# Causal attention without mask matmuls: VectorE adds the mask while it takes the maxima, GpSimd zeroes the weights of later keys

## The chip, the cores and the metric

The kernel runs on one core of one Trainium2 chip. The metric is the device time of one execution in microseconds (us), and lower is better. The core has five engines with a queue each: TensorE (PE, matmuls; PEld is its loading of weights), VectorE (DVE), ScalarE (ACT), GpSimd (POOL) and SyncE (SP, which issues most of the DMAs). Engines wait for each other only through semaphores. Matmul results go to PSUM, of which there are eight banks of 128 x 512 f32; everything else that is computed on lies in SBUF.

## What is computed

The reference is a model of four layers, each an attention-like mixer and a feed-forward part, on 4 sequences of 512 tokens with 128 channels. The change concerns the attention of the second layer (16 heads of 8 channels), which is causal: a query sees its own key and the earlier ones. It is softmax attention, with scale = 8 ** -0.5:

```
x = _layernorm(x + _L1_attn_ref(x, L1_attn_q_heads, L1_attn_k_heads, L1_attn_v_heads, L1_attn_output_proj), axis=-1)

scores[q, k] = (Q[q] . K[k]) * scale,   for k <= q alone
weights      = softmax over k of scores
output[q]    = sum over k of weights[q, k] * V[k],   then the output projection
```

The second block sums the attention up; the first line is the reference's own. The third and the fourth layer have attentions of the same size without causality (one with a bias by distance, one with an additional key).

## The kernel before

The stream of attention work is laid out in **units**: a unit is one sequence and four heads, so there are 16 units in each of the three attentions. A unit has eight **jobs** (128 jobs in all), each for one tile of 128 queries or keys and two of the four heads. Work is written out in **slots** t from -14 to 133. In slot t the engines' queues get:

- *maxima of job t + 14* (`maxima`): TensorE multiplies 128 queries (tile `qt`) by the keys up to the end of that tile, for two heads, into two PSUM banks (line 849). VectorE reduces both banks at once to the negated maximum of each row (line 1663, tile `negm`). The maxima are taken from coarser bf16 parts and only keep the exponentials in range.
- *turned maxima*, once a unit: GpSimd splits the maxima of a unit in a high and a low bf16 part (lines 2508 and 2510, `max_rows`), TensorE transposes them (line 859), VectorE copies the result to SBUF (line 1677), and a DMA from GpSimd's queue (line 2535, `row_of_maxima`) puts them as two rows into the query operands, so that the score matmul subtracts the maximum itself.
- *scores of job t* (`scores`): TensorE multiplies 128 keys (tile `kt`) by the queries from that tile on, one matmul a head (line 876). Keys lie on the partitions, queries along the bank. ScalarE takes the exponential of each head (line 1299) into the SBUF tile `PB`.
- *values*, in odd slots (`values`): TensorE multiplies the weights of the key tile of the jobs t - 3 and t - 2 by V with a column of ones, four heads side by side (line 892), accumulating over the four key tiles in bank 7. After the fourth, ScalarE copies the bank out (line 1312), TensorE turns it (line 900), and VectorE divides by the sum (lines 1693 and 1695, `output`).

Causality is done on TensorE. Where a product touches the diagonal tile, a further matmul of the identity (`b_ident`) by a 128 x 128 mask of 0 and -1e30 adds the mask to the bank: `b_causal_qk` after the maxima's matmuls (line 852, two a job), and `b_causal_kq` after each score matmul (line 879, two a job). The masks are loaded and cast to bf16 by GpSimd at the start of the kernel (`half_masks`, line 2274). `b_causal_kq` and `b_alibi_kq` have both the line 879; the latter belongs to the third layer's attention.

The maxima, the turned maxima and the outputs share a **ring** of two entries of two banks each (banks 0 to 3): the use number n needs the entry of use n - 2 freed by VectorE (semaphore `ring_free`; TensorE counts with `ring_filled`). The scores go round three banks (4 to 6), freed by ScalarE's exponentials (`exped`). `PB` is double buffered by key tile: ScalarE waits for the values two key tiles back (`valued`).

Each engine's queue is in order, and what stands in it is decided by the slots alone. In the last third of the stage other work is woven in by tables of slots (`inside1`): projection and normalisation of the three sequences that are done, the routing of their tokens to experts on VectorE, and on GpSimd scatters of token rows to DRAM by indirect DMA (lines 2342 and 2355), one a slot in the slots 93 to 100 and 105 to 112, with a copy at slot 104 that waits for the first eight (line 2348), and again from slot 125. The normalisation's inverse root is GpSimd's too (lines 2230 and 2232).

## Time and profile before

| | |
|---|---|
| median of 3 timed runs | 1177.18 us (1175.18 to 1180.2) |
| span of the profiled execution | 1195.9 us |
| difference of the two | 18.7 us |
| busy, share of the span | PE 85%, DVE 65%, ACT 55%, POOL 30% |
| chain of work that ended last, by engine | PE 67%, DVE 14%, ACT 8% |
| masks' matmuls in that chain (lines 879 and 852) | 3% and 2% |
| mean granted TensorE clock | 0.916 |

For the profiled execution the profile gives no time but its span, from the first to the last instruction. It is longer than the timed runs. All durations that are read from the trace belong to the profiled execution. In the rows, times are in us from the start of the span, unless marked ns; a group of instructions is named by its line in the kernel, its engine and operation, and what it writes and reads.

### The profile page before, as it was taken

To read this page: it belongs to the slowest core of one execution; us is meant where nothing else is said; L and a number is where in the kernel's file an instruction comes from. 1 tells how busy PE (TensorE), PEld (TensorE's weight loads), DVE (VectorE), ACT (ScalarE), POOL (GpSimd) and SP (SyncE) were. 2 spreads that over 40 slices of the span, in tenths; PEclk is the share of its full clock that TensorE was granted. 3 is DMA by queue.
4 is the path that set the end of the run, shared out by engine and by line. 5 is a ranking of instruction groups with operands and counts; after the bars stand their busy time and mean duration, and the time that the engine had idled before them with its cause. 6 is when DMAs were issued, how large, how long until landed. Compare 5 with 4: busy or idle time off the path is not lost.

```text
span 1195.9 us, 18814 instructions
## 1 busy us (share of the span) xinstructions
PE 1013.1 (85%) x6456; PEld 502.9 (42%) x6517; DVE 779.4 (65%) x1614; ACT 662.2 (55%) x1282; POOL 363.6 (30%) x587
## 2 busy tenths in 40 slices
PE   5599789999979899456999999798999998876993
PEld 2267534544436566332333333485323232233551
DVE  5966486768733300388888885429888889646565
ACT  4664536655544345152777777582477776753341
POOL 7535411101532244320000002210112223556554
PEclk9799779999988899865999999898799999999897
DMA  5910224334611120233333220003333423212232
GB/s 142 181 46 1 94 86 144 126 113 129 168 38 36 55 67 18 65 95 126 100 117 125 65 79 5 1 1 126 112 119 119 134 89 96 63 33 62 56 87 80
DMA packets 98374, 101.70 MB, mean 85 GB/s; under 512 B 13354, under 2 KB 80571, under 8 KB 98199
## 3 DMA queue, kind: packets, MB, share of 16 engines
q1 hardware_dynamic: 86169, 89.28, 25.3%
q0 software_dynamic: 6432, 8.18, 2.4%
q10 hardware_dynamic: 5680, 3.04, 0.9%
q8 instruction: 53, 0.87, 0.3%
q14 instruction: 40, 0.33, 0.1%
HBM read 66.60 MB, written 38.09 MB: 88 GB/s over the span
## 4 chain that ended last, share of the span: by engine, by line
PE 67%; DVE 14%; ACT 8%; issue 5%; DMA 3%; another core or an unknown queue 1%; POOL 1%; SPq 0%; ACTq 0%; DVEq 0%; POOLq 0%
PE PS L892 13%; PE PS L876 12%; PE PS L849 8%; PE PS L698 6%; PE PS L703 6%; DVE negm L1663 5%; PE PS L1170 4%; PE PS L1053 3%; PE PS L879 3%; PE PS L1047 2%; PE PS L852 2%; ACT arena L1299 2%; PE PS L900 2%; PE PS L1186 2%; ACT arena L1226 1%
## 5 line engine op out<-in xcount | busy, mean ns | idle before, releaser
L1299 ACT ACTIVATE arena<-PS 128x512 f32<-128x512 f32 (+3 forms) x768 | 363.0, 549 | 190.6 <-PE PS L879 121.8
L1663 DVE TENSOR_REDUCE negm<-PS 128x2 f32<-128x1024 f32 (+3 forms) x384 | 405.2, 1088 | 94.3 <-PE PS L849 46.1
L876 PE MATMUL PS<-arena 128*128 128x512 bf16 (+3 forms) x707 | 221.1, 363 | 12.1 <-ACT arena L1299 8.0
L892 PE MATMUL PS<-arena,VPAD 128*32 128x512 f32 (+3 forms) x1536 | 187.7, 559 | 0.1
L849 PE MATMUL PS<-arena 32*128 32x512 bf16 (+3 forms) x768 | 144.3, 376 | 33.1 <-DVE negm L1663 27.4
L849 PEld LDWEIGHTS PS<-arena 32*128 32x128 bf16 x768 | 36.3, 91 | 216.7 <-DVE negm L1663 112.9
L876 PEld LDWEIGHTS PS<-arena 128*128 128x128 bf16 x768 | 69.9, 98 | 123.5 <-issue 57.3
L2508 POOL CAST nmp<-negm 128x16 bf16<-128x16 f32 x48 | 9.3, 195 | 363.9 <-DVE negm L1663 244.1
L698 PE MATMUL PS<-arena,W 128*128 128x512 f32 x144 | 83.2, 711 | 11.5 <-ACT arena L1217 9.0
L703 PEld LDWEIGHTS PS<-W,arena 128*128 128x128 f32 x640 | 81.0, 206 | 13.8 <-issue 6.3
L703 PE MATMUL PS<-W,arena 128*128 128x128 f32 x640 | 82.8, 291 | 3.3 <-DVE arena L1607 3.0
L1170 PE MATMUL PS<-VPAD,arena 128*128 x92 | 53.3, 663 | 11.4 <-DVE arena L2174 5.5
L2535 POOL DMA_DIRECT2D arena<-mT x48 | 30.7, 639 | 101.1 <-DVE mT L1677 78.9
L1937 DVE TENSOR_TENSOR arena<-PS,arena 128x512 f32<-128x512 f32 x8 | 5.5, 692 | 84.2 <-PE PS L1053 84.2
L879 PE MATMUL PS<-b_alibi_kq,b_ident 128*128 128x128 bf16 x256 | 56.9, 222 | 4.0 <-issue 2.2
L2473 POOL DMA_INDIRECT rows_y<-arena,name x46 | 46.6, 1013 | 37.4 <-DVE arena L2187 17.9
L1407 ACT ACTIVATE arena<-PS,eb 128x320 f32<-128x320 f32 x64 | 33.8, 527 | 39.9 <-PE PS L1047 38.0
L2391 POOL DMA_INDIRECT rows_y<-arena,back x40 | 39.2, 981 | 54.6 <-DVE arena L1940 40.0
L879 PE MATMUL PS<-b_causal_kq,b_ident 128*128 128x128 bf16 x256 | 52.5, 224 | 2.8 <-issue 2.1
L1217 ACT COPY arena<-PS 128x512 f32<-128x512 f32 x39 | 22.7, 587 | 48.8 <-PE PS L694 45.3
L1047 PE MATMUL PS<-arena,VPAD 128*128 128x320 f32 x128 | 44.2, 472 | 3.4 <-ACT arena L1402 1.7
L698 PEld LDWEIGHTS PS<-arena,W 128*128 128x128 f32 x144 | 29.3, 225 | 41.9 <-issue 26.0
(334 smaller groups left out, 1541.3 us busy)
## 6 DMA issues: line engine op xcount, KB each, us to landing
arena<-score_q SPq DMA_DIRECT2D x48, 288.0 KB
arena<-score_k SPq DMA_DIRECT2D x48, 288.0 KB
arena<-max_parts SPq DMA_DIRECT2D x48, 256.0 KB
max_parts<-arena SPq DMA_DIRECT2D x36, 256.0 KB, 2.9
score_k<-arena SPq DMA_DIRECT2D x36, 128.0 KB
score_q<-arena SPq DMA_DIRECT2D x12, 384.0 KB
arena<-rows_y SPq DMA_DIRECT2D x16, 256.0 KB, 4.3
arena<-slots SPq DMA_DIRECT2D x46, 65.0 KB
```

The lines of the kernel that those rows point to most:

```text
L698: pe.matmul(bank(b), w, x, start=True, stop=True).then_inc(*T.did(c, name))
L703: mm = pe.matmul(PS[:, b, j * D:(j + 1) * D], lhs(f, j), rhs(f), start=(f == 0), stop=(f == nf - 1))
L849: mm = pe.matmul(PS[:, b + i, 0:nk], MQ[s][rows, qt * P:(qt + 1) * P], MK[s][rows, 0:nk], start=True, stop=True)
L876: mm = pe.matmul(PS[:, b, q0:S], OK[s][:, r, kt * P:(kt + 1) * P], OQ[s][:, r, q0:S], start=True, stop=True)
L879: mm = pe.matmul(PS[:, b, kt * P:(kt + 1) * P], bf["ident"][:], bf[o["kq"]][:], start=False, stop=True, skip_group_check=True)
L892: mm = pe.matmul(PS[32 * r:32 * r + 32, 7, q0:S], VP[:, u, kt, r, :], PB[:, kt % 2, r, q0:S], start=(kt == 0), stop=True, skip_group_check ...
L1047: pe.matmul(PS[:, (L.A, L.B)[h], 0:HALF], W1E[:, e, n * P:(n + 1) * P], L.exT[:, h * HALF:(h + 1) * HALF], start=True, stop=True).then_inc ...
L1170: pe.matmul(bank(2 * (t % 3) + 1), xT3[t % 4], WE3[:, bass.ds(experts[t] * 768, 512)], start=True, stop=True).then_inc(multiplied3, 1)
L1299: act.activation(PB[:, kt % 2, r, q0:S], PS[:, 4 + use % 3, q0:S], ACT.Exp, scale=slope(u % G, r) if o["slope"] else 1.0).then_inc(exped, 1)
L1663: vec.tensor_reduce(negm[:, u % 2, 2 * rp:2 * rp + 2, qt], PS[:, 2 * (use % 2):2 * (use % 2) + 2, 0:nk], AX.X, ALU.max, negate=True).then_ ...
L2391: pool.indirect_dma_start(rows_y, bass.IndirectOffsetOnAxis(ap=lanes[k].back[:, r, j:j + 1], axis=0), lanes[k].ey[:, j, :], None, bounds_c ...
L2473: pool.indirect_dma_start(rows_y, bass.IndirectOffsetOnAxis(ap=name3[:, i:i + 1], axis=0), y3[i], None, bounds_check=2 * B * S - 1, oob_is ...
```

## The change

The mask matmuls of the causal attention go, both kinds, and with them the masks `b_causal_kq` and `b_alibi_qk` (the latter was loaded and cast but not used by any matmul). In their place:

- **VectorE.** For each of the two heads of a job of maxima, one combined instruction (`tensor_tensor_reduce`) reads the head's PSUM bank and the mask `b_causal_qk`, adds them, multiplies by -1, writes the result back to the same bank and keeps the minimum, which goes to `negm`. The mask tile is now 512 columns wide: 384 of zeros ahead of the 128 of the diagonal tile, and its last `nk` columns are used. As it is built, each combined instruction is followed by a second one that writes the kept minimum, so four instructions stand where one stood.
- **GpSimd.** After the two exponentials of a job, an `affine_select` sets the weights of later keys to zero in the diagonal tile of `PB`, for both heads at once (128 x 2 x 128 f32). It waits for the exponentials (`exped`) and signals `selected`; the value matmuls of the causal attention wait for `selected` in place of `exped`. In a slot it stands behind the unit's `max_rows` and `row_of_maxima` and ahead of `inside1`.

```diff
--- before.py
+++ after.py
@@ -72,7 +72,7 @@
 BEHIND_TILES = {20: range(0, 3), 21: range(3, 6), 22: range(6, 8)}
 RES = float(1.0 / np.sqrt(2.0))
 EPS32 = float(np.finfo(np.float32).eps)
-NEG = -1.0e30
+NEG, FAR = -1.0e30, 3.0e38
 NCOMBO = 72
 NLIN = 9
 UNITS = B * G
@@ -305,10 +305,10 @@
         s1w, s2w = view(arena, lanes[0].tail, [512]), view(arena, lanes[1].tail, [4, D])
         eb2 = [view(arena, lanes[2 + e // 4].tail + D * (e % 4), [D]) for e in range(E)]
 
-        masks = ("causal_kq", "causal_qk", "alibi_kq", "alibi_qk", "tri")
+        masks = ("causal_qk", "alibi_kq", "tri")
         cst = {n: view(VPAD, 2048 + P * i, [P]) for i, n in enumerate(masks)}
         cst["ident"], cst["headmean"] = sb("c_ident", [P, P])[:], sb("c_headmean", [P, P])[:]
-        bf = {n: sb("b_" + n, [P, P], BF16) for n in ("ident",) + masks}
+        bf = {n: sb("b_" + n, [P, S if n == "causal_qk" else P], BF16) for n in ("ident",) + masks}
         ident = cst["ident"]
         rank, slopes, qscale2 = sb("rank", [P, E]), sb("slopes", [P, H]), sb("qscale2", [P, 1])
         ones, onesb = sb("ones", [P, P]), sb("onesb", [P, P], BF16)
@@ -377,8 +377,8 @@
         image_rows, blank_rows = sem("image_rows"), sem("blank_rows")
         max_row = [sem(f"max_row{s}") for s in range(NB)]
         ring_filled, ring_free, scored, exped = (sem(n) for n in ("ring_filled", "ring_free", "scored", "exped"))
-        valued, evacuated, max_high, max_low, inverted = (
-            sem(n) for n in ("valued", "evacuated", "max_high", "max_low", "inverted"))
+        valued, evacuated, max_high, max_low, inverted, selected = (
+            sem(n) for n in ("valued", "evacuated", "max_high", "max_low", "inverted", "selected"))
         void_low, void_max, void_sum, void_exp, void_part, void_added = (
             sem(n) for n in ("void_low", "void_max", "void_sum", "void_exp", "void_part", "void_added"))
         token_in = sem("token_in")
@@ -386,9 +386,9 @@
         expert_x, returned, expert_w = [sem(f"expert_x{k}") for k in range(B)], [sem(f"returned{k}") for k in range(B)], sem("expert_w")
         out_done = sem("out_done")
 
-        ATT = [dict(causal=True, kq="causal_kq", qk="causal_qk", lin=False, slope=False, void=False),
-               dict(causal=False, kq="alibi_kq", qk=None, lin=True, slope=True, void=False),
-               dict(causal=False, kq=None, qk=None, lin=False, slope=False, void=True)]
+        ATT = [dict(causal=True, kq=None, lin=False, slope=False, void=False),
+               dict(causal=False, kq="alibi_kq", lin=True, slope=True, void=False),
+               dict(causal=False, kq=None, lin=False, slope=False, void=True)]
 
         def max_job(t):
 
@@ -847,10 +847,6 @@
                     for i in range(2):
                         rows = slice(32 * (2 * rp + i), 32 * (2 * rp + i) + 32)
                         mm = pe.matmul(PS[:, b + i, 0:nk], MQ[s][rows, qt * P:(qt + 1) * P], MK[s][rows, 0:nk], start=True, stop=True)
-                    if o["qk"]:
-                        for i in range(2):
-                            mm = pe.matmul(PS[:, b + i, qt * P:(qt + 1) * P], bf["ident"][:], bf[o["qk"]][:],
-                                           start=False, stop=True, skip_group_check=True)
                     mm.then_inc(ring_filled, 1)
 
                 def turned(u):
@@ -885,7 +881,10 @@
                     q0 = kt * P if o["causal"] else 0
                     if a == 0 and block == 0:
                         pe.wait_ge(*PO.at(WHOLE, "vp1"))
-                    pe.wait_ge(exped, score_use[a, 2 * block + 1] + 2)
+                    if o["causal"]:
+                        pe.wait_ge(selected, 2 * block + 2)
+                    else:
+                        pe.wait_ge(exped, score_use[a, 2 * block + 1] + 2)
                     if kt == 0 and a * UNITS + u > 0:
                         pe.wait_ge(evacuated, a * UNITS + u)
                     for r in range(R):
@@ -1660,6 +1659,15 @@
                     if job % 8 == 0 and k >= 2:
                         vec.wait_ge(max_low, k - 1)
                     vec.wait_ge(ring_filled, use + 1)
+                    if o["causal"]:
+                        if job == 0:
+                            vec.wait_ge(*PO.at(WHOLE, "bf"))
+                        for i in range(2):
+                            found = PS[:, 2 * (use % 2) + i, 0:nk]
+                            t = vec.tensor_tensor_reduce(found, found, bf["causal_qk"][:, S - nk:S], -1.0, FAR, ALU.add, ALU.min,
+                                                         accum_out=negm[:, u % 2, 2 * rp + i, qt:qt + 1])
+                        t.then_inc(ring_free, 1)
+                        return
                     vec.tensor_reduce(negm[:, u % 2, 2 * rp:2 * rp + 2, qt], PS[:, 2 * (use % 2):2 * (use % 2) + 2, 0:nk],
                                       AX.X, ALU.max, negate=True).then_inc(ring_free, 1)
 
@@ -2272,10 +2280,11 @@
                 pool.wait_ge(*PO.at(WHOLE, "half"))
 
             def half_masks():
+                pool.memset(bf["causal_qk"][:, 0:S - P], 0.0)
                 pool.wait_ge(mask_in, 16 * len(masks))
                 pool.wait_ge(ident_in, 16)
                 for n in bf:
-                    t = pool.tensor_copy(bf[n][:], cst[n])
+                    t = pool.tensor_copy(bf[n][:, S - P:S] if n == "causal_qk" else bf[n][:], cst[n])
                 t.then_inc(*PO.did(WHOLE, "bf"))
 
             def ternary_weights():
@@ -2534,12 +2543,20 @@
                     pool.wait_ge(*ring_freed[ring_use[a, "turned", u]])
                     pool.dma_start(OQ[s][KR:KR + 2].rearrange("a r (t q) -> a (r t) q", t=CT), mT[:, s, :]).then_inc(max_row[s], 16)
 
+                def own_keys_only(job):
+                    kt, rp = job % 8 // 2, job % 2
+                    own = PB[:, kt % 2, 2 * rp:2 * rp + 2, kt * P:(kt + 1) * P]
+                    pool.wait_ge(exped, score_use[a, job] + 2)
+                    pool.affine_select(own, own, [[0, 2], [1, P]], ALU.is_ge, no_weight, base=0, channel_multiplier=-1).then_inc(selected, 1)
+
                 def slot(t):
                     job = max_job(t)
                     if job is not None and job % 8 == 7:
                         max_rows(job // 8)
                     if turned_unit(t) is not None:
                         row_of_maxima(turned_unit(t))
+                    if o["causal"] and exp_job(t) is not None:
+                        own_keys_only(exp_job(t))
                     if o["void"] and exp_job(t) is not None and t % 8 == 4:
                         void_parts(t // 8)
                     if a == 0:
@@ -2549,6 +2566,7 @@
 
                 return slot
 
+            no_weight = pool.to_reg(0.0)
             attend = [attention(a) for a in range(3)]
             start()
             layer0(attend[0])
@@ -2631,10 +2649,8 @@
     o["c_ident"] = np.eye(P, dtype=f)
     token = (P * np.arange(NT)[None, :] + i[:, None] - NOWHERE).astype(f)
     o["c_token_rows"] = np.ascontiguousarray(np.stack([token, token + B * S], 1))
-    o["c_causal_kq"] = np.where(k > q, NEG, 0).astype(f)
-    o["c_causal_qk"] = np.ascontiguousarray(o["c_causal_kq"].T)
+    o["c_causal_qk"] = np.ascontiguousarray(np.where(k > q, NEG, 0).astype(f).T)
     o["c_alibi_kq"] = np.minimum(k - q, 0).astype(f)
-    o["c_alibi_qk"] = np.ascontiguousarray(o["c_alibi_kq"].T)
     o["c_headmean"] = np.where(k // HD == q // HD, 1.0 / HD, 0).astype(f)
     o["c_tri"] = (k < q).astype(f)
     o["c_rank"] = np.tile(E - np.arange(E), (P, 1)).astype(f)
```

On VectorE, in the steady part of the stage, this stands for two jobs of 256 keys and the output that follows (`ISA` is the combined instruction or, without inputs, the one that writes its minimum). Before:

```order
L1663 TENSOR_REDUCE negm<-PS 128x2 x6
L1677 COPY mT<-PS 32x128
L1663 TENSOR_REDUCE negm<-PS 128x2 x2
L1693 RECIPROCAL rden<-PS 128x16
L1695 TENSOR_TENSOR arena<-PS,rden 128x4x32
```

Now:

```order
L1685 COPY mT<-PS 32x128
L1667 ISA PS,negm<-PS,b_causal_qk 128x256
L1667 ISA negm 128x1
L1667 ISA PS,negm<-PS,b_causal_qk 128x256
L1667 ISA negm 128x1
L1667 ISA PS,negm<-PS,b_causal_qk 128x256
L1667 ISA negm 128x1
L1667 ISA PS,negm<-PS,b_causal_qk 128x256
L1667 ISA negm 128x1
L1701 RECIPROCAL rden<-PS 128x16
L1703 TENSOR_TENSOR arena<-PS,rden 128x4x32
```

The two reductions between the copy of the turned maxima and the output have become eight instructions; nothing else moved there.

On TensorE, two slots of the steady part, without value matmuls. Before:

```order
L849 MATMUL PS<-arena 128x256 x2
L852 MATMUL PS<-b_causal_qk,b_ident 128x128 x2
L876 MATMUL PS<-arena 128x256
L879 MATMUL PS<-b_causal_kq,b_ident 128x128
L876 MATMUL PS<-arena 128x256
L879 MATMUL PS<-b_causal_kq,b_ident 128x128
```

Now:

```order
L849 MATMUL PS<-arena 128x256 x2
L872 MATMUL PS<-arena 128x256 x2
L849 MATMUL PS<-arena 128x256 x2
L872 MATMUL PS<-arena 128x256 x2
L899 MATMUL PS<-c_ident,arena 128x128 x4
```

The rows of before are one slot, those of now are two and the turning of an output behind them: a slot has four matmuls where it had eight.

On GpSimd, where it scatters token rows (slots 93 to 104, now from 96 on; `slots_x` is the DRAM tensor of the experts' tokens). Before:

```order
L2342 DMA slots_x<-X,scatter_to 5120x129 x4
L2508 CAST nmp<-negm 128x16
L2510 TENSOR_TENSOR nmp<-negm,nmp 128x16
L2342 DMA slots_x<-X,scatter_to 5120x129 x2
L2535 DMA arena<-mT 2x16x128
L2342 DMA slots_x<-X,scatter_to 5120x129 x2
L2348 COPY X<-token_rows 128x8
```

Now:

```order
L2351 DMA slots_x<-X,scatter_to 5120x129
L2517 CAST nmp<-negm 128x16
L2519 TENSOR_TENSOR nmp<-negm,nmp 128x16
L2550 AFFINE_SELECT arena<-arena 128x2x128
L2351 DMA slots_x<-X,scatter_to 5120x129
L2550 AFFINE_SELECT arena<-arena 128x2x128
L2351 DMA slots_x<-X,scatter_to 5120x129
L2544 DMA arena<-mT 2x16x128
L2550 AFFINE_SELECT arena<-arena 128x2x128
L2351 DMA slots_x<-X,scatter_to 5120x129
L2550 AFFINE_SELECT arena<-arena 128x2x128
L2351 DMA slots_x<-X,scatter_to 5120x129
```

A selection stands ahead of every scatter, and behind the split and the DMA of the maxima.

## Rows read from the trace of the kernel before

**Rows 1.** Three stretches: length, busy of PE, PEld, DVE, ACT, POOL; granted clock, DMA share, GB/s.
```profile
150.00:172.00 22.00, 16.74 (x87) 8.51 (x87) 21.29 (x52) 6.59 (x11) 4.80 (x8) 0.78 0.17 62
172.00:332.00 160.00, 152.94 (x1487) 75.50 (x1501) 114.96 (x230) 93.44 (x245) 32.26 (x63) 0.98 0.44 137
332.00:357.00 25.00, 19.12 (x186) 8.57 (x187) 8.81 (x39) 12.92 (x36) 7.28 (x10) 0.86 0.06 20
```
**Rows 2.** Waits from 180 to 350: us in total, times, longest.
```profile
PE PS L849 <- DVE negm L1663: 1.4, 4, 0.6
...
DVE negm L1663 <- PE PS L852: 28.1, 48, 1.4
...
ACT arena L1299 <- PE PS L879: 60.9, 67, 2.1
```
**Rows 3.** Chain that ended last, in order of time (start, us, what).
```profile
190.36 0.78 PE PS L892 x8
...
200.44 0.78 PE PS L892 x8
```
**Rows 4.** TensorE in order of time, one slot (start, us, group).
```profile
233.21 0.28 PE L852 MATMUL PS<-b_causal_qk,b_ident 128*128 128x128 bf16 x2
233.34 0.22 PE L876 MATMUL PS<-arena 128*128 128x128 bf16 x1
233.39 0.22 PE L879 MATMUL PS<-b_causal_kq,b_ident 128*128 128x128 bf16 x1
233.45 0.22 PE L876 MATMUL PS<-arena 128*128 128x128 bf16 x1
```
**Rows 5.** The same columns for one unit.
```profile
188.86:198.95 10.09, 10.02 (x103) 4.74 (x103) 7.19 (x12) 6.34 (x17) 1.02 (x4) 1.00 0.37 121
```
**Rows 6.** VectorE in order of time, around the turned maxima [idle before <-releaser].
```profile
197.66 0.21 DVE L1677 COPY mT<-PS 32x128 bf16<-32x128 bf16 x1 [0.35 <-PE PS L859]
198.95 1.46 DVE L1663 TENSOR_REDUCE negm<-PS 128x2 f32<-128x512 f32 x2 [1.08 <-PE PS L852]
```
**Rows 7.** VectorE's groups by line and form: busy us, mean ns | idle before.
```profile
L1663 DVE TENSOR_REDUCE negm<-PS 128x2 f32<-128x1024 f32 x288 | 340.5, 1221 | 67.7 <-PE PS L849 46.1 <-POOL nmp L2510 8.4 <-PE PS L852 6.2
...
L1537 DVE COPY VPAD<-PS 128x128 f32<-128x128 f32 x32 | 6.9, 279 | 3.1 <-PE PS L703 3.1
...
L1937 DVE TENSOR_TENSOR arena<-PS,arena 128x512 f32<-128x512 f32 x8 | 5.5, 692 | 84.2 <-PE PS L1053 84.2
...
L1940 DVE TENSOR_TENSOR arena<-PS,arena 128x128 f32<-128x128 f32 x8 | 2.3, 292 | 1.5 <-PE PS L1053 1.4
...
L1585 DVE MEMSET arena<- 128x8 f32 x4 | 0.3, 65 | 0.3
...
L1637 DVE RECIPROCAL rs<-va 128x4 f32<-128x4 f32 x4 | 0.7, 172 | 2.9 <-POOL va L2252 2.9
```
**Rows 8.** VectorE in order of time, in the ramp.
```profile
155.12 0.38 DVE L1511 BATCH_NORM_AGGREGATE mv<-bn 128x2 f32<-128x6 f32 x4
...
165.48 0.86 DVE L1537 COPY VPAD<-PS 128x128 f32<-128x128 f32 x4
```
**Rows 9.** GpSimd's groups by line and form: busy us, mean ns | idle before.
```profile
L2285 POOL TENSOR_SCALAR VPAD<-W,thr 128x512 f32<-128x512 f32 x2 | 3.5, 1774 | 1.1 <-DVE thr L1555 1.1
...
L2278 POOL CAST b_causal_qk<-VPAD 128x128 bf16<-128x128 f32 x1 | 0.3, 297 | 0.0
```
**Rows 10.** ScalarE and TensorE in order of time: longest exponentials and their value matmuls.
```profile
194.03 2.11 ACT L1299 ACTIVATE arena<-PS 128x512 f32<-128x512 f32 x4 [1.10 <-PE PS L879]
...
197.40 1.08 PE L892 MATMUL PS<-arena,VPAD 128*32 128x512 f32 x8
```
**Rows 11.** GpSimd in order of time, where it scatters.
```profile
310.93 0.97 POOL L2342 DMA_INDIRECT slots_x<-X,scatter_to  x1 [0.30 <-issue]
...
319.55 0.20 POOL L2348 COPY X<-token_rows 128x8 f32<-128x8 f32 x1 [4.38 <-DMA slots_x<-X,scatter_to]
```
**Rows 12.** The same columns as in rows 1, a later stretch.
```profile
980.00:1020.00 40.00, 33.21 (x208) 9.25 (x211) 36.54 (x78) 25.55 (x52) 16.18 (x27) 1.00 0.38 109
```

## Prediction

> **What bounds the kernel now.** I read the busy time by stretch first, then the waits, then single units of work. The change touches only the first attention stage. It lies between 150 and 357 us, in three stretches [rows 1]: a ramp (150 to 172) in which only maxima run, a steady stretch (172 to 332), and a tail (332 to 357) without maxima. Before and after these nothing moves but some preparation.
>
> In the steady stretch TensorE is busy 152.9 of 160 us, VectorE 115.0, ScalarE 93.4 and GpSimd 32.3 [rows 1]. Busy TensorE alone proves little, so the waits have to confirm it: VectorE waited 28.1 us for the mask matmul of line 852 and ScalarE 60.9 us for that of line 879, while TensorE's maxima waited 1.4 us for VectorE [rows 2]. So TensorE's own order sets the pace. The pace is read off the chain of work: the same group of value matmuls comes 10.08 us later, one unit (8 slots) later [rows 3]. 114 of the 128 slots are in this stretch, so 14.25 units.
>
> **What leaves TensorE.** In a slot the pair of line 852 starts at 233.21 and the next matmul at 233.34: 0.13 us [rows 4]. Each matmul of line 879 holds the next one for 0.055 us (233.39 to 233.45), two a slot: 0.11 us. That is 0.24 us a slot, 1.9 us a unit, and TensorE alone would need 8.2 us for a unit instead of 10.1. If nothing else came in the way that would be 14.25 x 1.9 = 27 us. It does not follow, for three engines have to keep up.
>
> **VectorE's maxima.** In one unit, from 188.86 to 198.95, VectorE is busy for 7.2 us and idle for 2.9: eight maxima, a copy of the turned maxima and the two steps of an output [rows 5]. The order shows what takes the place of one reduction over two heads: four instructions, two heads of the combined form, each followed by one that writes the accumulated value to negm. The number of elements stays; what is new is three more fixed costs a job. Now a job pays one, about 0.155 us (1.22 us for 1024 elements at 1.04 ns each, the slope of the two-input rows [rows 7]). The trace has no instruction of the new kind, so I bound it. Upper end: a two-input instruction that reads PSUM takes 692 ns for 512 elements and 292 for 128, so 159 ns fixed, and a small arithmetic one 172 ns [rows 7]; twice their sum is 0.66 us a job, +0.51. Lower end: instructions with no wait between them start closer together. Four copies out of PSUM of 279 ns fill 0.86 us [rows 7, 8], so they start 0.19 apart, 0.13 of it elements: 0.06 fixed. With the smallest instruction of the engine, 65 ns [rows 7], that is 2 x 0.125 = 0.25 a job, +0.10. The new ones also write the sums back to PSUM, which no VectorE row does; I see no way in which that makes them cheaper than this. I take **+0.20 a job**: 0.06 for each head, 0.075 for each read of the accumulator (four small aggregations fill 0.38 us, so they start 0.075 apart [rows 8]) and one end that nothing hides, 0.08: 0.35, less 0.155. It stands near the lower end because these rows, like the four new instructions, follow each other without a wait.
>
> The Trainium skill, VectorE: DVE Perf Modes, on the TRN2 errata, gives a PSUM source 120 cycles and an SBUF one 58 beside the elements at 0.96 GHz; an estimate by it is 0.37 us a job, +0.22, and the sum below would hardly move. Its section on the DRAIN says to keep the number of instructions low, which speaks against this change; that four stand for one here is in the order, and no row of before shows their price.
>
> So a unit costs VectorE 7.2 + 8 x 0.20 = 8.8 us. That it waits cannot all be recovered: behind the copy of the turned maxima it stands still for 1.08 us, since in TensorE's order the longest value matmuls lie before the next maxima [rows 6]; 0.13 of it is mask. 8.8 + 0.95 + 0.3 for the other gaps (1.8 us now, most of which TensorE's spare 1.9 us takes away) is 10.05 us. That is the pace of before: the saving of TensorE becomes waiting for VectorE, **and the steady units give 0 us**. Break-even is at +0.20 a job; each 0.05 more is 0.4 us a unit.
>
> **The ramp.** There VectorE is busy 21.3 of 22 us [rows 1], so nothing hides what is added: 14 jobs x 0.20 = **+2.8 us**.
>
> **VectorE's other work.** In the steady stretch it has 115.0 - 14.25 x 7.2 = 12 us of other work (normalisation, routing). Beside a waiting TensorE it has cost little; once VectorE sets the pace it lies on the path; but the matmuls that belong to it (16 us beyond the units' 14.25 x 10.1) now come to lie beside VectorE. I take **+2 us** of the possible 0 to 6.
>
> **GpSimd's selection.** A new instruction a job over 256 elements. No row shows one; a cast takes 297 ns for 128, a comparison 1774 ns for 512 [rows 9]. Ends: 0.35 us (little over the cast) and 0.95 us (the comparison, halved and a little more); I take 0.5, under twice the cast, for part of the cast's time is fixed. The Trainium skill, GPSIMD Engine Reference, section 7, gives compare-and-select bodies about 1 to 2 cycles an element, an estimate of 0.2 to 0.45 us and a dispatch; by it the next term shrinks to about 4.
>
> The value matmuls now wait for it. In a plain unit the longest exponentials end at 196.14 and their value matmuls start at 197.40 [rows 10]: 1.26 us, of which some 0.6 are masks that go. 0.5 us and two hand-overs just fit. Not so where GpSimd scatters. Each scatter takes it 1.3 us with its issue gap (0.97 and 0.30) [rows 11], and 16 of them stand one to a slot, in two groups of eight, with selections now between. 1.3 + 0.55 = 1.85 us a slot against 1.26 that a slot takes: 0.6 x 8 = 4.7 a group. The first group also holds a cast and a subtraction (0.5) and a DMA issue (0.69); the second these and a normalisation (1.3). That is 5.9 and 7.2 us, less some 2.5 each by which it may fall behind before value matmuls two slots later wait, and less 2 in all because in this piece GpSimd already waits (among it 4.4 us waiting for a scatter [rows 11]). **+6 us**; +3 at 0.35 us, +13 at 0.95.
>
> **Rest.** In the tail TensorE saves 14 x 0.11 = 1.5 us and each value block waits for a selection more: **-1 us**. Two casts of 0.3 us go [rows 9], a memset comes, and two small loads go: 0, they have the time of the first layer as cover, and were it gone they are worth under 0.5. TensorE idles more; its granted clock was 1.00 where it was busy only 33.2 of 40 us [rows 12], so I book no clock.
>
> **Sum.** 2.8 + 0 + 2 + 6 - 1 = +9.8 us. The profiled execution's span is 1195.9 us, 18.7 above the median of the timed runs; I carry the difference in microseconds: 1177.2 + 9.8 = **1187.0 us**.
>
> **Rivals.** (1) *TensorE stays the limit.* If a job costs VectorE only +0.10 and a selection 0.35, a unit falls to 7.2 + 0.8 + 1.25 = 9.25 us, 14.25 x 0.85 = -12; ramp +1.4, other work +1, scatters +4 (they meet a faster pace), tail -1: -7, **1170 us**. For it: VectorE's 2.9 us of waiting. Against: it needs the lower end twice. It decides below about +0.13 a job. (2) *The fixed costs are full ones.* At +0.35 a job a unit takes 7.2 + 2.8 + 1.25 = 11.3 us: 14.25 x 1.2 = 17, ramp 5, other work 3, scatters 5, tail -1: +29, **1206 us**; at +0.51 it would be near 1226. For it: with the write to PSUM and an accumulator to be read there is a reason for each instruction to wait for the one ahead. Mine and this one differ in size; it decides from +0.30. (3) *Offsets meet*: the selection is short and the scatters' backlog is absorbed, VectorE as I say: 2.8 + 0 + 0 + 0 - 1, **1179 us**, no change. (4) *The change doesn't do what it says*: the order shows no mask matmul left in the stage, so I give this none.
>
> **Chances.** My forecast (1181 to 1197) 0.42; rival 1 0.24; rival 2 0.22; rival 3 0.12. Both signs hold a good part, so the forecast's own range is 1181 to 1197 and the whole range is 1169 to 1212: it leaves out the quick half of rival 1 and the slow quarter of rival 2. About 0.5% (5.9 us) is what a measurement of this kernel can tell from no change. Faster by more: 0.25 (rival 1 and a little). Within: 0.17 (rival 3 and my forecast's lower edge). Slower: 0.58.
>
> **What would show it.** Right: line 852 and 879 gone, the combined instruction at about n x 1.04 + 60 to 160 ns; the reductions wait less than 28 us and TensorE's maxima (line 849) wait for VectorE by over 10 us in the stretch where it was 1.4; units at about 10 us; value matmuls waiting for GpSimd in the slots with scatters and scarcely elsewhere. Wrong: a unit near 9 us with TensorE still busy 95% (rival 1), a unit over 11 (rival 2), a selection of 1 us that holds every block of value matmuls, or a granted clock below 0.9 in the steady stretch.

## The result, and the profile after

The changed kernel takes 1183.56 us (median of 12 runs, 1178.89 to 1185.96) where before takes 1176.95 (12 runs, 1171.03 to 1180.2): ratio 1.0053, interval 1.0034 to 1.0072. That is 6.6 us slower; the forecast was 9.8. (Every ratio here is to runs of before made alongside, whose median was between 1176.7 and 1177.4 us each time.) The profiled execution of after took 1183.67 us, with a span of 1182.3.

First the rows that answer to [rows 1] and [rows 5]: three stretches of the stage, and one unit (length; busy PE, PEld, DVE, ACT, POOL with counts; granted clock, DMA share, GB/s).

```profile
150.00:172.00 22.00, 13.84 (x59) 6.89 (x59) 21.76 (x85) 6.59 (x11) 4.99 (x8) 0.78 0.19 62
172.00:332.00 160.00, 140.21 (x1015) 52.21 (x1030) 129.53 (x569) 90.20 (x241) 73.94 (x170) 0.91 0.44 136
332.00:357.00 25.00, 19.29 (x179) 8.12 (x179) 11.57 (x52) 14.36 (x40) 16.91 (x31) 0.91 0.08 23
188.60:198.35 9.75, 8.87 (x71) 3.13 (x71) 8.12 (x36) 6.56 (x19) 4.30 (x12) 1.00 0.38 113
```

TensorE is no longer busy throughout: 140 of 160 us where it was 153, and 8.87 of 9.75 in a unit where it was 10.02 of 10.09. Over the three stretches VectorE has 162.9 us of work where it had 145.1. The granted clock of the long stretch fell from 0.98 to 0.91; the section on the clock comes back to that.

The waits of after answer to [rows 2] (170 to 352 us; in total, times, longest).

```profile
PEld PS L849 <- DVE negm L1667: 27.1, 41, 2.3
DVE PS L1667 <- PE PS L849: 24.4, 31, 2.0
...
PE PS L849 <- DVE negm L1667: 8.9, 15, 1.9
```

TensorE's maxima now wait for VectorE (8.9 us of matmuls, 27.1 us of their weight loads, which partly overlap other matmuls; 1.1 and 10.3 us in the same window of the second profile of before), and VectorE still waits 24.4 us for TensorE, where it waited 30.5. Each waits for the other. The chain that ended last, in order of time (start, us, what), shows the same within one unit, and answers to [rows 3].

```profile
191.52 0.78 PE PS L891 x8
192.61 0.57 DVE PS L1667
...
196.72 0.59 DVE PS L1667
197.94 0.37 POOL arena L2550
198.35 1.06 PE PS L891 x8
...
208.09 1.06 PE PS L891 x8
```

A unit takes 9.74 us. About half of it the chain runs over VectorE's maxima, and from there over GpSimd to the longest value matmuls. Why GpSimd stands in it is seen in its queue (start, us, what, [idle before]):

```profile
197.44 0.20 POOL L2517 CAST nmp<-negm 128x16 bf16<-128x16 f32 x1 [1.18 <-DVE negm L1667]
197.72 0.22 POOL L2519 TENSOR_TENSOR nmp<-negm,nmp 128x16 bf16<-128x16 f32 x1
197.89 0.77 POOL L2550 TENSOR_SCALAR_AFFINE_SELECT arena<-arena 128x256 f32<-128x256 f32 x2
```

GpSimd splits the maxima ahead of the selection. Its cast waits 1.18 us for VectorE, although the exponentials that the selection is for had ended at 196.76; the value matmuls of 198.35 so wait for VectorE's maxima by way of GpSimd. Whether that costs the unit anything, the run without a selection tells further down.

**Where the time went.** A block is the value matmuls of one key tile and four heads, four to a unit and 64 in all, dated by its first matmul. Block 0 ends the ramp, 44 lies just ahead of the scatters, 60 opens the last unit. A plain unit is one without other work woven in; there are five, from blocks 4, 8, 12, 24 and 28. A second profile of before (label e0_before_again; span 1172.2, 1173.91 us) serves as the comparison, for the first, with its span of 1195.9, was an unusually long execution.

| us | before, second profile | after | difference |
|---|---|---|---|
| kernel's start to the stage's first matmul | 143.6 | 147.6 | +4.0 |
| from there to block 0 | 29.2 | 30.7 | +1.6 |
| block 0 to 44 | 121.1 | 118.3 | -2.8 |
| block 44 to 60 | 44.6 | 51.7 | +7.0 |
| block 60 to the next layer's first expert matmul | 55.6 | 55.4 | -0.2 |

The first line is not of the change: it lies between 143.1 and 148.0 in the fourteen profiles, and is 147.6 in the first profile of before. The others sum to +5.6 us, against 6.6 measured. Each is one execution of each kernel, and how far they repeat is seen where kernels have the same instructions: up to slot 91 after and e3 below are the same, with 118.3 and 119.2 us for blocks 0 to 44, and the two profiles of before have 121.0 and 121.1 there. Blocks 44 to 60 repeat less well: 44.6 and 50.8 us in the two profiles of before. So the +7.0 is not safe by itself; the pairs of kernels below have to bear it out.

### The profile page after: what moved, and what is told of

Same layout as the page of the kernel before. It is cut to its first block, busy times and chain, and to the rows that moved or that the text cites. A ratio compares the mean times of both kernels' runs of the same rounds, so it can differ in the third digit from the quotient of the medians.

```text
span 1182.3 us, 18301 instructions
## 1 busy us (share of the span) xinstructions
PE 990.8 (84%) x5944; PEld 475.9 (40%) x6005; DVE 796.7 (67%) x1998; ACT 660.2 (56%) x1282; POOL 415.2 (35%) x714
## 4 chain that ended last, share of the span: by engine, by line
PE 63%; DVE 17%; ACT 9%; issue 5%; POOL 3%; DMA 3%; another core or an unknown queue 0%; SPq 0%; ACTq 0%; POOLq 0%; DVEq 0%
PE PS L872 12%; PE PS L891 12%; PE PS L849 7%; PE PS L703 7%; PE PS L698 6%; DVE PS L1667 4%; PE PS L1169 4%; DVE negm L1671 4%; PE PS L1052 3%; ACT arena L1298 2%; PE PS L1046 2%; PE PS L1185 2%; PE PS L899 2%; ACT arena L1406 2%; ACT arena L1225 1%
## 5 line engine op out<-in xcount | busy, mean ns | idle before, releaser
L1671 DVE TENSOR_REDUCE negm<-PS 128x2 f32<-128x1024 f32 x256 | 302.2, 1221 | 54.0 <-PE PS L849 44.3
L1667 DVE CUSTOM_DVE_ANT_0 PS<-PS,b_causal_qk 128x128 f32<-128x128 f32 (+3 forms) x256 | 117.7, 524 | 24.8 <-PE PS L849 24.4
L872 PEld LDWEIGHTS PS<-arena 128*128 128x128 bf16 x768 | 64.1, 98 | 136.8 <-issue 63.9
L2550 POOL TENSOR_SCALAR_AFFINE_SELECT arena<-arena 128x256 f32<-128x256 f32 x128 | 52.1, 412 | 71.3 <-ACT arena L1298 68.8
L1216 ACT COPY arena<-PS 128x512 f32<-128x512 f32 x39 | 22.7, 587 | 50.8 <-PE PS L694 47.0
L2238 POOL TENSOR_SCALAR va<-mv 128x4 f32<-128x4 f32 x32 | 8.2, 257 | 117.7 <-DVE mv L1510 116.8
```

The source lines that it names most:

```text
L872: mm = pe.matmul(PS[:, b, q0:S], OK[s][:, r, kt * P:(kt + 1) * P], OQ[s][:, r, q0:S], start=True, stop=True)
L1667: t = vec.tensor_tensor_reduce(found, found, bf["causal_qk"][:, S - nk:S], -1.0, FAR, ALU.add, ALU.min, accum_out=negm[:, u % 2, 2 * rp + ...
L1671: vec.tensor_reduce(negm[:, u % 2, 2 * rp:2 * rp + 2, qt], PS[:, 2 * (use % 2):2 * (use % 2) + 2, 0:nk], AX.X, ALU.max, negate=True).then_ ...
L2550: pool.affine_select(own, own, [[0, 2], [1, P]], ALU.is_ge, no_weight, base=0, channel_multiplier=-1).then_inc(selected, 1)
```

## Experiments

### Either half alone, and the selection only where there are no scatters

> The kernel before, for a second look at its trace. Its first profiled execution spans 1195.9 us, 18.7 above the median of the timed runs, while the changed kernel's spans 1182.3 against a median of 1183.6. If the first look at before was a long one, this one spans about 1176 us, the causal stage's last value matmuls end some 3 to 6 us earlier than in the first look, and the steady units are again 10.08 us apart.

It took 1173.91 us. Its times are in the table above.

e1_vector_alone is after with TensorE adding the masks of keys again and no selection on GpSimd:

```
-    dict(causal=True, kq=None, lin=False, ...)
+    dict(causal=True, kq="causal_kq", lin=False, ...)
-    if o["causal"]:
-        pe.wait_ge(selected, 2 * block + 2)
-    else:
-        pe.wait_ge(exped, score_use[a, 2 * block + 1] + 2)
+    pe.wait_ge(exped, score_use[a, 2 * block + 1] + 2)
-    if o["causal"] and exp_job(t) is not None:
-        own_keys_only(exp_job(t))
```

> The VectorE part alone: the maxima are masked inside the combined instruction, the scores are masked by TensorE as before and GpSimd selects nothing. Theory A (the loss sits with GpSimd, where selections stand among scatters): a unit costs VectorE 7.2 + 8 x 0.12 = 8.2 us and TensorE 9.05, so units of about 9.6 us, 7 us gained in 14.25 units, 2 lost in the ramp, 2 in other work: 0.997 of before (1174 us). Theory B (the loss sits with VectorE's extra fixed costs): units of 10 us or more, ramp +3, other work +4: 1.005 or more (1183 us).

Measured: 1177.76 us (12 runs), ratio to before 1.0002 (0.9983 to 1.0020). The time lies between the two theories (0.997 and 1.005) and the interval holds neither; the unit is about that of theory A.

e2_gpsimd_alone is before with only the key masks moved: `kq=None`, the selection and its wait as in the change, maxima as before.

> The GpSimd part alone: later keys' weights are zeroed by the selection, the maxima are masked by TensorE and reduced in one instruction a job as before. Theory A: TensorE saves 0.88 us a unit, 12 us, but the scatters with selections among them cost 6 us and the last scatters another 3 behind the stage: between 0.997 and 1.003 of before. Theory B: the 12 us arrive nearly in full: 0.991 (1166 us).

Measured: 1178.18 us (12 runs), ratio 0.9996 (0.9975 to 1.0017), as theory A has it.

e3_select_until_92 is after, but from slot 92 on TensorE adds the masks of keys and GpSimd selects nothing:

```
+    def by_gpsimd(t):
+        return t < 92
-    if o["causal"] and exp_job(t) is not None:
+    if o["causal"] and exp_job(t) is not None and by_gpsimd(t):
         own_keys_only(exp_job(t))
```

> The changed kernel with the selection only up to slot 91, that is in none of the slots in which GpSimd scatters; from slot 92 on TensorE masks the scores as before. The maxima stay with VectorE throughout. Theory A: 36 slots lose 0.11 us of TensorE each (4 us), the scatters' 6 us and the 3 behind the stage come back: 0.995 of the changed kernel and about 1.000 of before (1177 us). Theory B: no gain, 1.000 to 1.003 of the changed kernel, 1.005 to 1.008 of before.

Measured: 1178.0 us (12 runs), ratio 1.0003 (0.9983 to 1.0022), theory A again. So the selections from slot 92 on cost about 5.6 us by the medians (1183.56 - 1178.0), 3.7 of it seen in the one profile between blocks 44 and 60 (47.9 against 51.7). Two more pairs further down differ in the same way and agree: e2 against e10 (1178.18 - 1172.23, 6.0 us) and e8 against e11 (1179.75 - 1174.92, 4.8 us). In the profiles blocks 44 to 60 are shorter in both, by 1.7 and 4.5 us.

The unit, in the same columns as above: first of e1, then of e2.

```profile
198.39:208.10 9.71, 9.38 (x87) 3.78 (x86) 8.27 (x37) 6.20 (x18) 1.02 (x3) 1.00 0.50 173
```
```profile
238.32:248.00 9.68, 9.38 (x87) 3.80 (x86) 7.13 (x12) 6.22 (x19) 4.27 (x11) 1.00 0.44 138
```

This is the surprise of the study. Either half alone brings a unit from 10.09 to about 9.7 (the middle one of the five plain units; single ones take up to 10.15 in e1 and 10.76 in e2), with TensorE 9.38 busy. Both halves together take a further 0.5 us off TensorE's busy time and give nothing: 9.74. Over blocks 0 to 44 the same: 118.4 and 117.3 for the halves, 118.3 for both. The second half of the saving bought no time.

GpSimd's queue where the scatters are, first of after, then of e3:

```profile
312.41 1.00 POOL L2351 DMA_INDIRECT slots_x<-X,scatter_to  x1 [0.18 <-issue]
313.44 0.41 POOL L2550 TENSOR_SCALAR_AFFINE_SELECT arena<-arena 128x256 f32<-128x256 f32 x1
314.03 0.99 POOL L2351 DMA_INDIRECT slots_x<-X,scatter_to  x1 [0.17 <-issue]
```
```profile
308.97 1.01 POOL L2355 DMA_INDIRECT slots_x<-X,scatter_to  x1 [0.30 <-issue]
310.28 0.97 POOL L2355 DMA_INDIRECT slots_x<-X,scatter_to  x1 [0.30 <-issue]
```

With selections between them the scatters stand 1.6 us apart, without 1.3.

### What holds a unit at 9.7 us

My next theory was the ring: VectorE idles 1.1 us behind the copy of the turned maxima, because the longest value matmuls precede the next maxima on TensorE. e4_values_behind_maxima moves that block behind the next slot's maxima:

```
     if job is not None:
         maxima(job)
+    if put_off:
+        values(put_off.pop())
+    if o["causal"] and block is not None and turned_unit(t) is not None and max_job(t + 1) is not None:
+        put_off.append(block)
+        block = None
```

> Kernel after, with one value block in each unit moved on TensorE: in the slot where the maxima are turned, its value block is issued behind the next slot's maxima instead of ahead of them. The turned maxima sit in the ring of two buffers, so VectorE has to copy them before TensorE can fill that buffer again. Theory A (what is left of TensorE's gain is held back there: VectorE idles about 1 us once a unit until the next maxima stand, and this is now on the path): the unit of 9.74 us falls by about half of that idle time, to 9.2 to 9.4, 14 units give 5 to 7 us, and the time is 1177 to 1179, ratio to after 0.995. Theory B (the unit is held by something else, the exponentials or VectorE's own work of 8.1 us with its other waits): the unit stays at 9.7 and the time at 1183 to 1184, ratio to after 1.000; the idle time moves to another place on VectorE.

Measured: 1186.5 us (7 runs), ratio to before 1.0078 (1.0048 to 1.0108): 3 us slower than after. The idle time at that place fell from 1.1 us to between 0 and 0.2, and the plain unit stayed at 9.7. Where other work is woven in, the move hurts. TensorE in order of time, one such place of e4:

```profile
231.03 0.39 PE L849 MATMUL PS<-arena 32*128 32x256 bf16 x2 [1.33 <-DVE negm L1674]
```

TensorE stands for 1.33 us for VectorE with the value matmuls, which it could have done, behind the waiting instruction; in after they fill that gap (at 228.76, for 1.06 us), and 0.48 us of waiting are left. Behind the stop the granted clock of e4 is at 0.50 (232 to 234), and the same value matmuls take 1.94 us. Theory A falls: the wait of VectorE there was no cause of the unit's length.

> Kernel before, with the same value block moved in the same way. Both theories have TensorE as the bound of the unit there (10.07 us busy of 10.09), so the order of its own work gives it nothing: 1177, ratio 1.000, unit 10.1. If it is faster by more than 0.3%, the unit of before was not held by TensorE's work alone.

The same move in before: 1181.76 us (10 runs), ratio 1.0038 (1.0013 to 1.0062), also worse; neither theory had that. Blocks 0 to 44 take 124.1 us for 121.1, with a plain unit of 10.33, and here the clock is at 1.00 throughout. So before's own order is the better one; where the moved block costs it the 0.24 us a unit stays open.

e7_selection_twice issues the selection twice a job, the second after the first:

```
+    pool.affine_select(own, own, ..., no_weight, base=0, channel_multiplier=-1).then_inc(selected_once, 1)
+    pool.wait_ge(selected_once, job + 1)
     pool.affine_select(own, own, ..., no_weight, base=0, channel_multiplier=-1).then_inc(selected, 1)
```

> Kernel after, with the selection issued twice for each job, the second after the first has ended: 0.4 us more on GpSimd per slot, 128 times. Theory A (GpSimd's selection costs nothing in steady units, where GpSimd has 4.3 us of work in 9.75, and its full length in the slots with scatters, where it stands in one row with them): blocks 0 to 44 as in after within 1 us, blocks 44 to 60 longer by 28 slots x 0.4 to 0.5 = 11 to 14 us, the time 1195 to 1198. Theory B (the selection's latency, from the exponentials to the value block, counts in each unit too): 2 to 5 us more in blocks 0 to 44, the time about 1200. Theory C (the scatter stretch is slower for another reason, such as GpSimd and VectorE holding each other up): under 5 us more in blocks 44 to 60, time under 1190.

Measured: 1200.72 us (4 runs), ratio 1.0203 (1.0158 to 1.0247). Blocks 0 to 44 take 5.0 us more than after, blocks 44 to 60 11.9 more. That is theory B: a longer selection is paid in the plain units too, 0.5 to 0.7 us in a unit of eight. The 11.9 us are not the second selections alone: the granted clock of that stretch is 0.68, where after has 0.78.

The next two leave a part of the work out. e8_no_mask_on_maxima is after with the one plain reduction a job of before and no mask on the maxima at all:

```
-    if o["causal"]:
-        if job == 0:
-            vec.wait_ge(*PO.at(WHOLE, "bf"))
-        for i in range(2):
-            ...
-        t.then_inc(ring_free, 1)
-        return
     vec.tensor_reduce(negm[...], PS[...], AX.X, ALU.max, negate=True).then_inc(ring_free, 1)
```

> Kernel after, but VectorE takes the maxima with the one plain reduction per job of before and nobody masks them: the mask of maxima is left out, so a query's maximum may be that of a later key of its own tile (the weights and their sum are shifted alike; the selection still zeroes later keys). TensorE's work is that of after (8.87 us a unit), VectorE's that of before (7.18), GpSimd's that of after. Theory V (VectorE's longer maxima are what keeps the unit at 9.75 instead of about 9.0): unit 9.0 to 9.2, blocks 0 to 44 shorter by 5 to 7 us, with the ramp's 1.5 us the time is 1175 to 1177. Theory S (the selection, which stands between the exponentials and the value matmuls, keeps it): unit stays 9.6 to 9.8, only the ramp's 1.5 us is won, the time 1181 to 1182.

Measured: 1179.75 us (10 runs), ratio 1.0014 (0.9997 to 1.0031), between the two theories. e9_no_selection is after without the selection, values waiting for `exped` alone:

> Kernel after without the selection, and the value matmuls wait for the exponentials alone: nobody zeroes the weights of later keys in a tile's own square, that part of the computation is left out. TensorE's and VectorE's work are those of after. Theory V: unit stays 9.6 to 9.8; only the scatter stretch gains its 5 to 7 us: 1176 to 1178. Theory S: unit 9.0 to 9.2, a further 5 to 7 us: 1170 to 1172. If neither this nor the run without the mask of maxima brings the unit under 9.5, each of the two alone is enough to hold it, or it is held by a third thing that both share (order of TensorE's own queue).

Measured: 1175.4 us (10 runs), ratio 0.9980 (0.9965 to 0.9994), a little under theory V. Two plain units of e8, then two of e9:

```profile
186.96:196.17 9.21, 8.70 (x71) 3.09 (x70) 6.90 (x11) 6.17 (x19) 4.25 (x11) 1.00 0.36 113
196.17:205.76 9.59, 8.73 (x71) 3.11 (x70) 7.03 (x11) 6.18 (x19) 4.24 (x11) 1.00 0.51 176
```
```profile
194.82:204.42 9.60, 8.90 (x70) 3.21 (x71) 7.99 (x35) 5.95 (x18) 1.01 (x3) 1.00 0.49 171
204.42:214.68 10.26, 8.87 (x71) 3.12 (x70) 8.43 (x37) 6.09 (x18) 1.01 (x3) 1.00 0.45 149
```

The five plain units of e8 take 9.22, 9.59, 9.46, 9.85 and 9.89 us, those of e9 9.73, 9.59, 10.26, 10.03 and 9.76. What each waits for is in TensorE's order of time. The first two rows are from the second unit of e8 above, the other two from e9, one from each unit above:

```profile
202.02 0.59 PE L872 MATMUL PS<-arena 128*128 128x512 bf16 x2 [0.32 <-issue]
...
205.49 0.34 PE L872 MATMUL PS<-arena 128*128 128x384 bf16 x1 [0.54 <-ACT arena L1298]
```
```profile
203.65 0.23 PE L849 MATMUL PS<-arena 32*128 32x128 bf16 x2 [0.60 <-DVE negm L1664]
...
210.94 0.59 PE L872 MATMUL PS<-arena 128*128 128x512 bf16 x2 [0.85 <-issue]
```

The rows with "issue" are the first score matmuls of a unit. In the kernel they wait for `max_row`, the DMA that puts the turned maxima into the query operands, and in the trace they start 0.09 us after it has landed, in four of e8's five plain units. That DMA took 3.8 to 5.8 us from its issue to its landing in the plain units of after, e1, e2, e8, e9 and e11. It is the third thing that e9's text asks for, and it explains the spread: in e8 the waits there are 0, 0.32, 0.19, 0.57 and 0.62 us, and each unit is 9.22 us and that wait, within 0.06.

So theory S falls: without a selection blocks 0 to 44 take 118.9 us, and 118.3 with it. The wait of the value matmuls by way of GpSimd costs the unit nothing at this length. Theory V holds for the larger part. Where the DMA does not hold a unit, it takes 9.2 us with the short maxima (e8, and e11 below) and 9.6 to 9.7 with the long ones (9.73 and 9.59 in e9, 9.74 in after), where TensorE's last maxima of the unit wait 0.6 us for VectorE. In after the DMA's wait is up to 0.44 us and hardly shows, since the wait for VectorE behind it gets shorter; in e8 it is paid in full. What is left in e8's shortest unit, 0.5 us over TensorE's 8.70, is a wait for ScalarE's exponentials (0.44). Where other work is woven in, VectorE's extra time counts as much: the unit from block 20 to 24 takes 11.90 us in after and 11.38 in e8, and blocks 0 to 44 take 118.3 and 114.9, 3.4 us.

### Repairs

e5_mixed_best is e3, with the move of e4, and TensorE masking the maxima in the ramp (`job < 14`) where VectorE takes the plain reduction.

> Three repairs at once, each where the trace of after showed a loss: the masks of keys are added by TensorE again from slot 92 on (the slots with scatters), the masks of maxima are added by TensorE again in the ramp (the first 14 jobs, where VectorE's maxima are the path), and the value block is moved behind the next maxima. If the block times add up: from after minus 5.5 (scatters, as measured with the first repair alone), minus 1.5 (ramp), minus 5 (value block, if theory A of that run holds) or 0 (if B): 1171.5 or 1176.5, ratio to before 0.995 or 1.000.

Measured: 1181.36 us (12 runs), ratio 1.0030 (1.0005 to 1.0054). A miss. The move, which cost 3 us in e4 and 5 in e6, is the likely reason, but the profile does not bear that out: against e3 it has a ramp shorter by 2.1 us, blocks 0 to 44 longer by 1.2 (120.4 against 119.2) and blocks 44 to 60 shorter by 0.6, and 4.4 us more behind block 60, where nearly all the instructions are the same. The cause stays open.

e10_gpsimd_alone_until_92 is e2 with the limit of e3. e11_no_mask_on_maxima_until_92 is e8 with that limit.

> Kernel before with GpSimd's selection for slots 0 to 91 alone; TensorE keeps the masks of maxima throughout and takes the masks of keys again from slot 92 on, where the scatters are. Block times of the runs with one part alone: ramp as before (29.2 against 29.0), blocks 0 to 44 117.3 against 121.1, blocks 44 to 60 as before. If they add up: 1173.5, ratio to before 0.997. If the scatter stretch gives back what the steady units gain, as it did with the selection throughout: 1177, ratio 1.000.

Measured: **1172.23 us** (6 runs, 1168.52 to 1174.49), ratio to before 0.9941 (0.9919 to 0.9963). The forecast was 1173.5. This beats both kernels.

> No mask on the maxima (left out, as in the run of that name), plain reductions, and GpSimd's selection for slots 0 to 91 alone, TensorE masking the keys from 92 on. Theory V: ramp as before, unit 9.0 to 9.2, scatter stretch at or under before: 1168 to 1171, ratio to before 0.993 to 0.995. Theory S: the unit stays at 9.7, the time is that of the selection alone with its end repaired, 1173 to 1175, ratio 0.997 to 0.998.

Measured: 1174.92 us (12 runs), ratio 0.9989 (0.9966 to 1.0011). The time is that of theory S, but three of its plain units come near theory V's (9.22, 9.37 and 9.46; the others 9.58 and 9.78). It is no faster than e10 although it leaves the mask of the maxima out. In the one profile of each it is ahead: blocks 0 to 60 take 161.3 us in e11, 165.9 in e10, and 165.8 in the second profile of before. The profile of e10 is the slowest of its six runs (1174.49). Of e10's gain it shows 2.9 us in blocks 0 to 44 (118.2 against 121.1; e2, with the same instructions there, 117.3). In blocks 44 to 60 its 47.8 us lie between the two profiles of before, 44.6 and 50.8, so where the other 2 us lie stays open.

## The clock in the scatter stretch

Blocks 44 to 60 carry the result, and half of what they show was not in the prediction. The same columns, one line each: before (second profile), e1, e9, after, e7.

```profile
293.90:338.53 44.63, 41.47 (x425) 20.76 (x424) 28.74 (x74) 26.51 (x72) 21.39 (x29) 1.00 0.49 128
```
```profile
297.22:342.41 45.19, 39.22 (x383) 18.09 (x381) 32.26 (x146) 26.38 (x72) 21.49 (x29) 1.00 0.50 130
```
```profile
293.76:341.44 47.68, 41.36 (x317) 16.74 (x316) 32.17 (x143) 26.15 (x72) 21.42 (x29) 0.89 0.45 121
```
```profile
296.67:348.33 51.66, 44.81 (x314) 17.04 (x317) 32.60 (x143) 26.53 (x72) 34.48 (x61) 0.78 0.40 111
```
```profile
302.21:365.72 63.51, 49.78 (x314) 18.46 (x317) 34.39 (x143) 27.10 (x72) 48.01 (x95) 0.68 0.32 90
```

After has 111 fewer matmuls than before and is busy 3.3 us longer, at a granted clock of 0.78 where before has 1.00; the other 3.7 of the 7.0 us are idle time of TensorE. What TensorE did before it fell is in stretches of 2 us of after:

```profile
306.00:308.00 2.00, 0.66 (x4) 0.28 (x4) 1.46 (x10) 1.93 (x5) 1.75 (x5) 1.00 0.71 152
308.00:310.00 2.00, 1.79 (x12) 0.48 (x13) 0.25 (x2) 0.00 (x0) 1.78 (x4) 0.81 0.85 246
310.00:312.00 2.00, 2.00 (x10) 1.14 (x8) 1.70 (x8) 1.32 (x4) 1.86 (x3) 0.50 1.10 270
```

and in the order of GpSimd and TensorE there:

```profile
306.49 0.99 POOL L2351 DMA_INDIRECT slots_x<-X,scatter_to  x1 [0.17 <-issue]
307.48 0.22 POOL L2517 CAST nmp<-negm 128x16 bf16<-128x16 f32 x1
307.79 0.22 POOL L2519 TENSOR_TENSOR nmp<-negm,nmp 128x16 bf16<-128x16 f32 x1
```
```profile
308.15 0.22 PE L855 MATMUL PS<-b_ident,nmp 128*32 128x128 bf16 x1 [0.97 <-POOL nmp L2519]
308.42 1.17 PE L891 MATMUL PS<-arena,VPAD 128*32 128x512 f32 x8
...
312.29 1.51 PE L891 MATMUL PS<-arena,VPAD 128*32 128x384 f32 x8
```

GpSimd has fallen behind by its selections, so the split of the maxima comes late; TensorE waits 0.97 us for it (busy 0.66 of 2 us), and then the granted clock goes from the 2.4 GHz level to the 1.2 GHz level (0.50) and stays there for some 12 us. (The stretch also opens at 0.50, from 296.7 to about 299.) Value matmuls that take 0.85 us in the plain unit take 1.51. Once more it waits from 328 to 330 (busy 0.49 of 2 us), this time 1.51 us for the selection itself, and the clock is at 0.50 until 336. A stop alone does not decide it. Before has waits in this stretch too (busy 1.11 of 2 us at 310, 0.91 at 328), and its clock stays at 1.00 in the second profile; in the first it was 0.56 from 336 to 340, after eight microseconds with 5.4 of busy time. And e1, first of the two below, stood still for 2 us and more at 1.00, where e9's clock fell after 1.04 and 0.68 of busy time in 2 us each:

```profile
312.00:314.00 2.00, 1.48 (x14) 0.54 (x10) 1.51 (x7) 0.89 (x3) 0.81 (x1) 1.00 1.06 279
314.00:316.00 2.00, 0.00 (x0) 0.00 (x0) 1.11 (x4) 0.00 (x0) 0.00 (x0) 1.00 0.39 104
316.00:320.00 4.00, 3.82 (x32) 2.13 (x32) 2.12 (x6) 2.71 (x6) 0.89 (x4) 1.00 0.82 229
```
```profile
310.00:312.00 2.00, 1.04 (x10) 0.50 (x6) 1.51 (x7) 0.58 (x1) 0.47 (x1) 1.00 0.81 205
312.00:314.00 2.00, 0.68 (x4) 0.22 (x4) 0.78 (x4) 0.21 (x1) 0.00 (x0) 1.00 0.57 181
314.00:318.00 4.00, 4.00 (x24) 2.41 (x22) 1.91 (x5) 2.33 (x5) 1.60 (x4) 0.58 0.81 225
```

The stops of e1 and e9, that of e10 below and that of before at 310 are the same one: the first score matmul of a unit waits 2.47, 1.98, 1.44 and 1.24 us for the DMA of the turned maxima, which took 6.0 to 6.5 us from issue to landing there.

e1 and e9 differ in this stretch only by TensorE's masks of keys. Without them it is *longer* by 2.5 us (47.7 against 45.2), with the clock at 0.89 instead of 1.00. It is tempting to say that the masks keep the clock, and e10 speaks against it. From slot 92 on its instructions are those of before, with all the masks on TensorE, and yet:

```profile
308.00:310.00 2.00, 0.66 (x6) 0.21 (x4) 1.23 (x1) 0.59 (x1) 0.00 (x0) 1.00 0.39 128
310.00:312.00 2.00, 1.90 (x11) 0.85 (x12) 0.32 (x1) 1.08 (x2) 0.19 (x1) 0.70 0.82 243
312.00:314.00 2.00, 2.00 (x15) 1.10 (x14) 0.91 (x1) 1.72 (x3) 0.41 (x2) 0.50 0.56 124
```

The second profile of before, e1 and e6, with the masks of keys on TensorE throughout, had a clock of 1.00 and 44.6 to 45.2 us, but the first profile of before had 0.93 and 50.8. It was 0.89 to 0.93 in e3, e5, e9, e10 and e11 (47.2 to 47.9), 0.90 in e2 (49.4), 0.78 to 0.83 in after, e4 and e8 (51.7 to 53.0), and 0.68 in e7 (63.5). So the clock was lowest where the selection stands among the scatters and TensorE waits most (idle 6.9 to 8.1 us in after, e4 and e8, and 13.7 in e7, against 3.2 to 6.5 in the others). Why the same stop is followed by a lower clock in one execution (e10) and not in another with the same instructions there (the second profile of before) is not shown.

## Why the prediction was right, and where its terms were off

The sign and the size came out (+6.6 measured, +9.8 forecast, range 1169 to 1212), but partly by luck, for the terms were off both ways: ramp and steady stretch together came out 6.0 us better than forecast, the scatters and the tail 1.8 worse. What carries the sign is the term of the scatters, and there the mechanism is shown: three pairs of kernels that differ in the selections from slot 92 on differ by 4.8 to 6.0 us. Of the signs set ahead, TensorE's maxima waited 7.0 us for VectorE in the stretch where it was 1.4, short of the 10 named (with their weight loads 22.5 more), and the granted clock of the steady stretch, 0.91, came close to the 0.9 that was to show me wrong.

- **The pace before** stood: in the second profile a unit takes 10.09 us, TensorE busy 10.08 of it.
- **What leaves TensorE**, 0.24 us a slot, is right where nothing waits: in before maxima and scores of one job fill 1.08 us (189.84 to 190.92, second profile), in after 0.85 (194.84 to 195.69). Yet its busy time fell only by 1.15 us a unit and not by 1.9, probably because a matmul that nothing follows shows its whole length, 0.22 us, where [rows 4] has the next one start after 0.055.
- **VectorE's price a job** was too high. Taken as +0.20, it measures +0.12 from the unit ((8.12 - 7.19) / 8) and +0.14 from the whole stage (17.8 / 128), just above my lower bound of +0.10. VectorE's rows show why:

```profile
195.29 0.14 DVE L1667 DVE_READ_ACCUMULATOR2_ANT negm<- 128x1 f32 x1
195.29 0.73 DVE L1667 CUSTOM_DVE_ANT_0 PS<-PS,b_causal_qk 128x512 f32<-128x512 f32 x1
195.93 0.14 DVE L1667 DVE_READ_ACCUMULATOR2_ANT negm<- 128x1 f32 x1
```

  The read of one accumulator (0.14 us long) starts together with the next head's instruction, and these start 0.645 us apart: 512 x 1.04 ns is 0.53, so both instructions of a head add 0.11. I had taken 0.06 + 0.075 for them. With +0.12 a job the end that nothing hides is left with 0.05 where I took 0.08. The estimate by the Trainium skill, VectorE: DVE Perf Modes, on the TRN2 errata, was +0.22 a job. For the length of one instruction the trace agrees with it: 0.727 us is 0.19 more than the elements, and its 120 and 58 cycles make 0.185, an estimate. For the price a job it does not: only 0.11 of it counts in a row, the rest overlaps the next instruction. (What the prediction quotes of the Trainium skill on the number of instructions stands in VectorE: DVE Perf Modes, in its rules for kernel authors, and not in its section on the DRAIN; four for one cost 0.12 to 0.14 us here.)
- **Steady units: 0 expected, a gain measured.** 9.74 us and not 10.05: by the value of +0.13 that I gave as the point of decision the case lay between my forecast and rival 1. But rival 1's unit of 9.25 did not come either. The step that failed is the sum for the unit: VectorE's work, a fixed 0.95 for the wait behind the turned maxima and 0.3 for the gaps. With the measured price it gives 7.2 + 0.96 + 1.25 = 9.4, and 9.74 came. The 0.95 as such was there (1.13 us at 199.67) but was no cause: moving it away won under 0.1 us a unit (e4). VectorE does hold the unit, with 0.6 us of waiting at another place, the unit's last maxima (e8 against after), and what hides behind it, the landing of a DMA, is not in the prediction at all.
- **VectorE's other work, +2**: the mechanism is there, since e8 gains 3.4 us over blocks 0 to 44, 2.6 of it in units with other work. Together with the gain of the units the stretch comes to -2.8 instead of +2.
- **The ramp**: +1.6 against +2.8, the price a job again (14 x 0.12 = 1.7).
- **GpSimd's selection** takes 0.412 us (0.5 taken):

```profile
L2550 POOL TENSOR_SCALAR_AFFINE_SELECT arena<-arena 128x256 f32<-128x256 f32 x128 | 52.1, 412 | 71.3 <-ACT arena L1298 68.8
```

  The estimate by the Trainium skill, GPSIMD Engine Reference, section 7, was 0.2 to 0.45 us for the elements and a dispatch on top; the 0.412 us of the whole instruction agrees if the elements take the lower part of that. That it just fits into the steady units is borne out from both sides: taken away it gives nothing there (e9), doubled it costs 0.5 to 0.7 us a unit (e7).
- **The scatters**: +7.0 against +6, but not by the backlog alone. A scatter and a selection stand 1.6 us apart, not 1.85, and TensorE's idle time in the stretch grew by 3.7 us only (51.66 - 44.81 against 44.63 - 41.47). The other 3.3 is busy time, at the slower clock, which outweighs the masks that went. That the size meets the forecast is luck: the waiting alone, which is all that the term counted, came to 3.7. *I book no clock* was the step that failed here: the row it rested on [rows 12] has a clock of 1.00 over 40 us with TensorE busy 33, and says nothing of a single stop of a microsecond.
- **Tail**: -0.2 against -1. **Sum**: of the 23.7 us by which the first profile of before is longer than the second, 4.0 lie ahead of the stage, 6.2 in the scatter stretch and 13 behind block 60; carrying differences in microseconds to the median was the right way.
